# The last pass of a four-layer graph network: another order of VectorE's operations in a step

## The reference

```python
f_src = feat @ W_src.T + b_src;  f_dst = feat @ W_dst.T + b_dst;  f_v = feat @ W_v.T + b_v
a = f_src[src] + f_dst[dst]
e = where(a >= 0, a, 0.2 * a)                    # leaky
seg_max = segment_max(e, dst)
ex = exp(e - seg_max[dst]);  seg_sum = segment_sum(ex, dst)
rst = segment_sum(f_v[src] * ex / seg_sum[dst], dst)
x = layernorm(x + rst)
```

## Time and profile before

| what | us |
|---|---|
| median of three runs | 4595.72 |
| the profiled execution, its own time | 4596.9 |
| its span on the core | 4592.8 |
| steady part of the last pass, from about | 3500 |
| to about | 4480 |
| mean granted clock of PE over the span | 0.89 of full speed |

### The profile page before, as it was taken

One profiled execution on the slowest core, in us unless ns is written; L12 is line 12 of the kernel. 1 busy time (PEld: TensorE's weight loads), 2 busy tenths in 40 slices (PEclk: granted clock), 3 DMA queues, 4 the chain that ended last, 5 costly groups with the idle time before them and its releaser, 6 DMA issues.

```text
span 4592.8 us, 103410 instructions
## 1 busy us (share of the span) xinstructions
PE 3703.2 (81%) x25659; PEld 3151.5 (69%) x25659; DVE 3297.4 (72%) x7523; ACT 2863.7 (62%) x7389; POOL 3272.3 (71%) x3433
## 2 busy tenths in 40 slices
PE   6888888887376666666879888888887999999996
PEld 5555555555376666666757777777777888888886
DVE  5766666666554444444668777777777999999998
ACT  3777767775532222222467666666656888888887
POOL 5777777775677777777657777777747777777772
PEclk8988888897587778777979999999989999999998
DMA  8888888884443333333122222222228878888882
GB/s 253 243 240 233 239 234 235 238 232 137 115 99 76 82 80 78 82 76 82 46 63 57 56 56 56 56 56 56 56 75 244 236 234 234 235 234 235 235 234 82
DMA packets 645300, 676.45 MB, mean 147 GB/s; under 512 B 126720, under 2 KB 511294, under 8 KB 645054
## 3 DMA queue, kind: packets, MB, share of 16 engines
q0 software_dynamic: 132928, 327.04, 27.2%
q1 hardware_dynamic: 511390, 347.67, 25.4%
q10 hardware_dynamic: 864, 0.39, 0.0%
HBM read 583.98 MB, written 89.08 MB: 147 GB/s over the span
## 4 chain that ended last, share of the span: by engine, by line
POOL 30%; issue 22%; PE 13%; DVE 12%; ACT 11%; DMA 7%; ACTq 2%; SPq 1%; DVEq 1%; POOLq 1%
POOL e_rows L877 21%; POOL xt L877 9%; PE banks L940 7%; ACT e_away L917 4%; DVE acc L964 4%; DMA xt<-up_t,e_index 3%; PE banks L1058 3%; DVE banks L1508 3%; ACT e_logit L1504 1%; ACT banks L1570 1%; DMA e_q_rows<-q_t 1%; PE banks L449 1%; ACTq L970 1%; ACT e_rows L1569 1%; ACT e_rise L1540 1%
## 5 line engine op out<-in xcount | busy, mean ns | idle before, releaser
L964 DVE TENSOR_TENSOR acc<-acc,banks 128x256 f32 x3328 | 1379.3, 414 | 887.8 <-PE banks L940 753.5
L877 POOL DMA_INDIRECT xt<-up_t,e_index x799 | 757.1, 948 | 243.5 <-issue 213.1
L877 POOL DMA_INDIRECT e_rows<-x_t,e_index x771 | 730.2, 947 | 246.6 <-issue 233.2
L877 POOL DMA_INDIRECT e_rows<-fsv_t,e_index x771 | 730.5, 947 | 235.1 <-issue 217.4
L877 POOL DMA_INDIRECT e_rows<-kv_t,e_index x771 | 730.3, 947 | 235.1 <-issue 223.7
L1200 ACT ACTIVATE e_rows<-banks,e_rows 128x128 f32<-128x128 f32 x832 | 237.0, 370 | 723.6 <-DMA e_rows<-x_t,e_index 467.4
L940 PE MATMUL banks<-e_sel,e_msg 128*128 128x128 f32 (+1 forms) x3328 | 653.1, 311 | 0.0
L1191 PE MATMUL banks<-e_w,xt 65*128 65x128 f32 x1664 | 271.4, 316 | 350.6 <-DMA xt<-in_attr_rows 345.6
L940 PEld LDWEIGHTS banks<-e_sel,e_msg 128*128 128x128 f32 (+1 forms) x3328 | 355.6, 147 | 262.0 <-issue 171.8
L917 ACT ACTIVATE e_away<-node_iota,local 128x128 f32<-128x128 f32 x1664 | 525.9, 388 | 0.0
L1191 PEld LDWEIGHTS banks<-e_w,xt 65*128 65x128 f32 x1664 | 247.5, 228 | 359.3 <-issue 314.0
(11 more groups left out here) (194 smaller groups left out, 7016.0 us busy)
## 6 DMA issues: line engine op xcount, KB each, us to landing
e_q_rows<-q_t SPq DMA_DIRECT2D x832, 64.0 KB
sel_d<-e_sel_t SPq DMA_DIRECT2D x208, 256.0 KB
e_sel_t<-sel_d SPq DMA_DIRECT2D x208, 256.0 KB
e_far<-fdst_t SPq DMA_DIRECT2D x832, 64.0 KB
e_near<-near_d SPq DMA_DIRECT2D x208, 128.0 KB
xt<-in_attr_rows SPq DMA_DIRECT2D x208, 128.0 KB, 3.4
e_resets<-reset_d SPq DMA_DIRECT2D x208, 128.0 KB
xt<-up_t,e_index POOLq DMA_INDIRECT x799
```

The source lines that it names most:

```text
L877: G.indirect_dma_start(out=self.rows[0:n, u, i, 0:self.width], out_offset=None, in_=self.table, in_offset=bass.IndirectOffsetOnAxis(ap=ind ...
L964: V.tensor_tensor(to, to, bank[n_bank][:, col:col + W].rearrange("p (k d) -> p k d", k=2), ALU.add).then_inc(self.s_added[i], 1)
```

## The change

The list of stages of `edges3` is written in another order. Only DVE's stages move: the lags, the waits, the operations and the order on PE, ACT, POOL and SP are as before.

```diff
-                    (2, leaky), (4, message), (5, ps.add(0, s_scaled)), (2, forward), (5, ps.add(1)),
-                    (2, backward), (5, ps.add(2)), (5, ps.add(3))])
+                    (5, ps.add(0, s_scaled)), (2, leaky), (5, ps.add(1)), (4, message), (5, ps.add(2)), (2, forward),
+                    (5, ps.add(3)), (2, backward)])
```

## The result

The changed kernel takes 4723.41 us (median of four runs, 4721.85 to 4725.83) against 4596.02 us of the kernel before: a ratio of 1.0282, 95% interval 1.027 to 1.0294. 4733 was predicted. The profiled execution took 4723.8 us, its span is 4719.8, 127.0 more than in the earlier trace rows.

The account below looks back on a forecast made before the run. DVE's step and a ring through ACT were both taken as 5.04, with POOL at 5.01. Addition 0 ahead of `leaky` lengthens the ring to 5.73: 4596.9 + 141 - 5 = 4733, range 4708 to 4785.

Parts of the forecast that it names:

- What bounds before: Last pass: DVE's step and a ring through ACT both 5.04, POOL's 5.01; a shorter DVE alone gives nothing.
- DVE's sum: DVE's operations of one last-pass step, start to start, with the merged pair of additions: 5.04 before the change.
- ACT's ring: Last pass: `leaky` on DVE, then `take_leaky` to `take` on ACT, back to `leaky`, with hand-overs: 5.04 a step.
- POOL's floor: Last pass: POOL's four gathers with only issue between them take 5.01 a step, 0.03 under the present step.
- (a), the pair: Additions 2 and 3 on DVE parted by `forward`: DVE's work shrinks 0.2 a step, at most 0.03 could arrive.
- (b), the other moves: `message`, `forward`, `backward` behind additions 1, 2, 3 on DVE: price nothing, smallest margin 0.5 at `forward`.
- (c), the ring: Addition 0 ahead of `leaky` on DVE puts `scaled` and hand-over into ACT's ring: step 5.73, 204 x 0.69 = 141 more.
- (d), the seams: Loop seams of the last pass, 0.28 each from DVE before, now hidden in idle time: 18 seams, -5, or 0.
- The sum: Whole kernel: 4596.9 + 141 - 5 = 4733.
- the clock rival: PE's clock falls in the last pass as its busy share drops to some 82%: 4803, chance 0.09.
- the second ring: `leaky`, `take_leaky` to `at_zero`, first half of `sums` on PE, addition 0, `leaky`: 5.20 in experiments; forecast only as slack.
- the first ring: `take`, `scaled`, addition 0, `leaky`, `take_leaky`, back to `take`, across ACT and DVE: forecast at 5.73 a step.

Follow-up runs that it names:

- two experiments that then showed 5.20: Changed kernel without `scaled` and addition 0's wait for it: 1.0002 of the kernel before; changed kernel with ACT's `take`, then `scaled` (lag 4), ahead of `exps`: 1.0061.
- a ring of 5.91 instead of 5.04: Changed kernel with one additional 128x128 copy on ACT between `take` and `scaled`: 1.005 of the kernel before, on the slower chips.

## Why the prediction was right

- *What bounds before.* Right, with both bounds shown: with `take` early the old order keeps 5.03 (DVE's sum), with every addition parted it keeps 5.04 (ACT's ring). Each alone holds the step; with both out of the way it is 4.97. The 5.01 taken as POOL's floor played no part in the result and was tested by no run.
- *(a), the pair.* Put at 0.2, measured 0.22; arrives nowhere in the changed kernel, as said.
- *(b), the other moves.* In the steady part no wait appeared at `message`, `forward`, additions 1 to 3 or `backward`; all of DVE's waits there, one in each of its 192 steps, are at addition 0.
- *(c), the ring.* Term by term: `take` to `scaled` 0.48, measured 0.47; `scaled` 0.30, 0.29; the hand-over to addition 0 0.20, 0.20; addition 0 to `leaky` 0.33, 0.34; `leaky` 0.70, 0.69; hand-over 0.03, 0.03; `take_leaky` to `take` 3.69, 3.69. Step 5.73, measured 5.715. The hand-over had the widest bounds (0.03 to 0.23), and the rows of register-addressed operations with two waits were the right ones to go by.
- *(d), the seams.* In the kernel before ten steps took 50.68 us, 0.28 more than ten times 5.04. In the changed kernel all steps of the loop are 5.71 or 5.72: the seams are hidden. Step by step the trace before has 17 seams of 0.25 on steps of 5.043, so 4.3 were saved where 5 were put.
- *The sum.* 136 was forecast, 127 came. The step accounts for 204 x 0.015 = 3 of the 9. Another 3.9 lie ahead of the pass: its first `leaky` started at 3470.4 before and at 3466.5 now, a difference of the passes before. Some 2.4 more come from one step near the pass's start, which took 7.43 in the kernel before (from 3483.8; DVE idled 2.31 ahead of `forward`, with no releaser shown) and 5.72 now. Such one-time differences no sum over steps could hold, and they happened to point the same way. From the first to the last `scaled` it is 1050.3 before and 1180.1 now, 129.8 more. The line L1552 of the changed kernel's trace (durations in ns, first and last start):

```profile
L1552 ACT ACTIVATE acc<-acc,e_shrink x208: 280/288/298, 3480.3 to 4660.4; - x104
```

- *The clock.* PE was busy 82%, as worked out, but the granted clock stayed 1.00 in the whole steady part, while pass three with 87% has 0.95. Nothing was lost to it. So the busy shares of two passes with other gaps said nothing sure about this one. By the rule of the Trainium skill, "TensorE: Matmul & The Clock Gate", Part 1, activity lifts the throttle; the trace agrees as far as that the clock stayed at its upper level with PE idle for about 1.0 once a step.
- *A margin named for another purpose.* The slack of 0.5 between the first half of `sums` and addition 0 was worked out for the clock rival. It is the second ring, 5.72 - 5.20 = 0.52. I had not seen that it closes to a ring, and so expected 5.01, or up to 5.05, of two experiments that then showed 5.20. The result was right without it only because the first ring was the longer.

## What to carry to other kernels

When an operation is moved ahead of another on one engine, look at what it waits for, and whether what now stands behind it feeds the engine that it waits for: two cross-engine waits that ran side by side become one ring, and its length is the sum of the terms, though every engine gets idler. Before pricing a saved wait on the busiest engine, close each ring through its neighbours from rows (end of one to start of the next): a tie within a few hundredths, as here, means that the saving can't arrive until both are shortened. And when a ring goes, price the next one too.

## What the runs showed of the hardware that was not expected

- A wait of DVE for its own neighbour is not free: an addition that waits for the addition right before it starts 0.53 after it; where another operation that needn't wait follows, that one starts after 0.33. Parting one pair was worth 0.22 a step. The Trainium skill, "VectorE: DVE Perf Modes", section "The DRAIN you can't avoid", says that a semaphore between two operations costs nothing extra, from a chain of eight copies; for these additions the runs don't agree.
- A 128x128 copy on ACT without a bias column took 0.30, 0.20 from start to start, against 0.39 and 0.29 for `distance`, which reads one at a place that a register gives; which of the two costs the 0.09 is not shown.
- The same program took 4592 to 4596 in the comparisons on the quick chips and 5843 to 5859 on three others, with 235 and 174 GB/s in the last pass, while the median durations of the instructions there agree within 0.02 (`leaky` 0.70 and 0.69, gather 0.95) and the packets' own time within 3%. What makes the difference is open. On the slow ones a ring of 5.91 instead of 5.04 cost 0.5%, where 5.72 costs 2.8% on the others.
